# Attention's weighted sums turned by DMA transposes of two 16-bit planes, taken apart and rejoined by GpSimd, instead of by TensorE

## The reference

```python
x = L0_attn_x                                   # (8, 1024, 256)
xn = _layernorm(x)
x = x + _L0_attn_ref(xn, W_kqv) + _L0_ffn_ref(xn, ...)

# attention, per batch b and head h
score = jnp.einsum('bhsd,bhnd->bhsn', q, k) / 16 + slope[h] * (n - s)
attn = jax.nn.softmax(score, axis=-1)
out = jnp.einsum('bhsn,bhnd->bhsd', attn, v)
```

## Time and profile before

| | |
|---|---|
| median of three runs | 2458.93 us |
| span of the profiled execution | 2465.2 us |
| TensorE busy | 2399.8 us, 97% |
| VectorE busy | 1899.4 us, 77% |
| ScalarE busy | 1561.3 us, 63% |
| GpSimd busy | 782.9 us, 32% |
| mean DMA rate | 93 GB/s |

### The profile page before, as it was taken

The page is one execution under the profiler, slowest core; times in us unless marked ns, Lnnn a source line. Parts: engine busy times, 40 slices in busy tenths (PEclk is TensorE's granted clock), DMA queues, the critical chain, the costliest instruction groups (busy, mean ns, idle before and its releaser), DMA issues.

```text
span 2465.2 us, 53774 instructions
## 1 busy us (share of the span) xinstructions
PE 2399.8 (97%) x19426; PEld 1490.7 (60%) x19426; DVE 1899.4 (77%) x2889; ACT 1561.3 (63%) x3276; POOL 782.9 (32%) x901
## 2 busy tenths in 40 slices
PE   8999999996999999989999999999999999999998
PEld 7888888886999999963333333333333333333333
DVE  6666566655556555568999999999999999999994
ACT  3333333333343333315888888888888888888888
POOL 2222323225242222210113333333333333333333
PEclk9999999997999999987999999999999999999999
DMA  6999877771332222232425343434344443435321
GB/s 189 185 166 176 172 129 148 140 120 35 87 98 76 76 75 76 77 74 47 84 49 103 62 88 71 87 72 84 74 79 80 74 85 72 87 67 91 64 58 40
DMA packets 177924, 229.05 MB, mean 93 GB/s; under 512 B 42828, under 2 KB 127436, under 8 KB 177656
## 3 DMA queue, kind: packets, MB, share of 16 engines
q1 hardware_dynamic: 153048, 172.02, 37.6%
q0 software_dynamic: 22448, 50.56, 8.6%
q10 hardware_dynamic: 2176, 3.02, 0.3%
HBM read 131.47 MB, written 93.66 MB: 91 GB/s over the span
## 4 chain that ended last, share of the span: by engine, by line
PE 52%; DVE 2%; DMA 1%; ACT 0%; issue 0%; SPq 0%; DVEq 0%; ACTq 0%
PE p_o L1430 23%; PE p L1418 18%; PE p L1405 9%; PE p L1442 1%; DVE part L1255 1%; DMA q_op<-m_row 1%; PE p L1411 1%; ACT probs L1379 0%; SPq L1144 0%; ACT o_sb L1367 0%; DVE neg L1263 0%; DVE att L1282 0%; DVE att L1302 0%; ACT o_t L1357 0%; DVE rec L1279 0%
## 5 line engine op out<-in xcount | busy, mean ns | idle before, releaser
L1255 DVE TENSOR_REDUCE part<-p 128x2 f32<-128x1024 f32 x1024 | 1237.8, 1221 | 79.9 <-PE p L1405 64.8
L1379 ACT ACTIVATE probs<-p 128x512 f32<-128x512 f32 x2048 | 1109.2, 596 | 159.6 <-PE p L1418 122.8
L1405 PE MATMUL p<-k_op,q_op 50*128 50x512 f32 x2048 | 757.2, 461 | 14.0 <-DVE part L1255 10.9
L1418 PE MATMUL p<-q_op,k_op 51*128 51x512 f32 x2048 | 756.5, 451 | 1.9 <-DMA q_op<-m_row 0.7
L1430 PE MATMUL p_o<-probs,v_op 128*32 128x256 f32 x8192 | 657.4, 392 | 5.1 <-ACT o_sb L1367 1.3
L1418 PEld LDWEIGHTS p<-q_op,k_op 51*128 51x128 f32 x2048 | 312.6, 186 | 417.3 <-ACT probs L1379 355.9
L1430 PEld LDWEIGHTS p_o<-probs,v_op 128*32 128x32 f32 x8192 | 163.3, 108 | 359.7 <-ACT probs L1379 285.0
L1405 PEld LDWEIGHTS p<-k_op,q_op 50*128 50x128 f32 x2048 | 307.0, 189 | 29.3 <-DVE part L1255 26.1
L1206 POOL TENSOR_TENSOR att<-o_t,rec 128x256 f32<-128x256 f32 x63 | 39.0, 618 | 809.1 <-DVE rec L1271 809.1
L828 POOL DMA_INDIRECT xe<-xn_scratch,ids x135 | 146.3, 1083 | 340.4 <-DMA ids<-lists_scratch 309.9
L921 ACT ACTIVATE gated_e<-p_gate 128x352 f32<-128x352 f32 x135 | 62.8, 465 | 194.9 <-PE p_gate L859 115.6
(11 more groups left out here) (186 smaller groups left out, 4052.7 us busy)
## 6 DMA issues: line engine op xcount, KB each, us to landing
k_op<-qk_scratch SPq DMA_DIRECT2D x192, 128.0 KB
q_op<-qk_scratch SPq DMA_DIRECT2D x192, 128.0 KB
yr_scratch<-x SPq DMA_DIRECT2D x135, 128.0 KB
qk_scratch<-k_op SPq DMA_DIRECT2D x32, 512.0 KB
qk_scratch<-q_op SPq DMA_DIRECT2D x32, 512.0 KB
v_scratch<-v_op SPq DMA_DIRECT2D x16, 1024.0 KB
v_op<-v_scratch SPq DMA_DIRECT2D x32, 512.0 KB
x<-in_x SPq DMA_DIRECT2D x16, 512.0 KB
```

Of the source, the lines that this page charges most:

```text
L1255: v.tensor_reduce(part[c_ % 2][:, kh, :, qb], p1[use % 2][:], AX.X, ALU.max, negate=True).then_inc(s["s1_read"], 1)
L1379: a.activation(probs[kb % 4][:, h], p2[use % 3][:], ACT.Exp).then_inc(s["s2_read"], 1)
L1405: return t.matmul(p1[use % 2][:, x], q_op[u][lo:lo + S1_ROWS, pair, q0:q0 + P], k_op[u][lo:lo + S1_ROWS, pair, kh * 512:(kh + 1) * 512], s ...
L1418: t.matmul(p2[use % 3][:], k_op[u][lo:lo + S2_ROWS, pair, kb * P:(kb + 1) * P], q_op[u][lo:lo + S2_ROWS, pair, half * HQ:(half + 1) * HQ], ...
```

## The change

The turn leaves TensorE and ScalarE. GpSimd's `split` copies the two 16-bit halves of each 32-bit value of `o_sb` into two planes `o_pl` (two copies of 128 x 512 values of 16 bits). SP's `turn_output` turns both planes with one DMA transpose (128 x 1024 values of 16 bits, 256 KB) into `o_x`. GpSimd's `rejoin` puts the halves together again in `o_t` (two copies of 128 x 272). VectorE's `invert` of a turn moves later, to the max unit at w = 1 or 17 of one half further on, and so does GpSimd's `normalise`, now one turn behind `split`. The arithmetic is the same.

```diff
-        OUT_COPY, OUT_TURN, OUT_SEEN = (1, 3), 13, 11
+        OUT_COPY, OUT_SEEN = (1, 3), 1
...
+            def turn_output(x_no):
+
+                sp.wait_ge(s["o_pl_ok"], x_no + 1)
+                if x_no >= 2:
+                    sp.wait_ge(s["o_out"], x_no - 1)
+                sp.dma_start_transpose(o_x[x_no % 2][:].rearrange("p t q r -> p (t q) r"),
+                                       o_pl[x_no % 2][:].rearrange("p t q -> p (t q)")
+                                       ).then_inc(s[f"o_x_in{x_no % 2}"], 16)
...
                 send_max(g, u, 1, use2(g, OWN_TURN) + 1)
+                if has_prev:
+                    turn_output(2 * g - 1)
                 if has_next:
                     send_max(g + 1, following(u, turn)[0], 0, use2(g, TURN_AT) + 1)
+                turn_output(2 * g)
...
+            def split(x_no):
+
+                u = x_no % 2
+                pool.wait_ge(s["o_ok"], 2 * x_no + 4)
+                if x_no >= 2:
+                    pool.wait_ge(s[f"o_x_in{u}"], 16 * (x_no // 2))
+                src = o_sb[u][:].bitcast(U16).rearrange("p (q t) -> p t q", t=2)
+                g_.tensor_copy(o_pl[u][:, 0], src[:, 0])
+                g_.tensor_copy(o_pl[u][:, 1], src[:, 1]).then_inc(s["o_pl_ok"], 1)
+
+            def rejoin(x_no):
+
+                u = x_no % 2
+                pool.wait_ge(s[f"o_x_in{u}"], 16 * (x_no // 2 + 1))
+                if x_no >= 2:
+                    pool.wait_ge(s["att_ok"], x_no - 1)
+                dst = o_t[u][:].rearrange("p q h c -> p (q h c)").bitcast(U16).rearrange(
+                    "p (q h c t) -> p t q h c", q=4, h=GH, t=2)
+                src = o_x[u][:].rearrange("p t q (h c) -> p t q h c", h=GH)
+                g_.tensor_copy(dst[:, 0], src[:, 0, :, :, 0:HD + 1])
+                g_.tensor_copy(dst[:, 1], src[:, 1, :, :, 0:HD + 1]).then_inc(s["o_out"], 1)
...
             for x_no in range(2 * GROUPS - 1):
-                normalise(x_no)
+                split(x_no)
+                if x_no:
+                    normalise(x_no - 1)
                 if x_no < NK:
                     last_batch(x_no)
                 if x_no >= NK - 1:
-                    pool.wait_ge(s["att_ok"], x_no + 1)
+                    pool.wait_ge(s["att_ok"], x_no)
                     combine(x_no - (NK - 1))
                 if NK - 2 <= x_no < first + NK - 2:
                     fetch(x_no - (NK - 2))
+                rejoin(x_no)
+            normalise(2 * GROUPS - 2)
...
-                        if w == half * (MAX_UNITS // 2) + OUT_SEEN and (half or has_prev):
-                            invert(2 * g + half - 1)
+                        if w == half * (MAX_UNITS // 2) + OUT_SEEN and has_prev:
+                            invert(2 * g + half - 2)
...
-                    elif n % HALF == OUT_TURN and (half or has_prev):
-                        turned_copy(*((g, 0) if half else (g - 1, 1)), use + 1)
...
-                    if l == OUT_TURN and (half or has_prev):
-                        turn_output(*((g, 0) if half else (g - 1, 1)), use + 1)
```

More of the change, by code:

```diff
@@ L19 @@
 I32 = mybir.dt.int32
+U16 = mybir.dt.uint16
 ALU = mybir.AluOpType
@@ L1069, in attend @@
         o_sb = [sb(f"o_sb{i}", [P, HQ]) for i in range(2)]
+        o_pl = [sb(f"o_pl{i}", [P, 2, HQ], U16) for i in range(2)]
+        o_x = [sb(f"o_x{i}", [P, 2, 4, P], U16) for i in range(2)]
         o_t = [sb(f"o_t{i}", [P, 4, GH, HD + 1]) for i in range(2)]
@@ L1083, in attend @@
                  "pool_c o_st0 o_st1 att_ok o_out base_in0 base_in1 yg_in0 yg_in1 fin_base fin_y "
-                 "dve_f fin_ok fin_st")
+                 "dve_f fin_ok fin_st o_pl_ok o_x_in0 o_x_in1")
         s = {n: sem("t_" + n) for n in names.split()}
@@ L1104, in turns_at @@
         def turns_at(g):
-            out = [OWN_TURN] + [h * HALF + OUT_TURN for h in range(2) if g or h]
-            return sorted(out + ([TURN_AT] if g < GROUPS - 1 else []))
+            return [OWN_TURN] + ([TURN_AT] if g < GROUPS - 1 else [])
         def use2(g, n):
@@ L1325, in group @@
                     last_terms()
+                    invert(2 * g)
                     dve.wait_ge(s["att_ok"], 2 * GROUPS - 1)
@@ L1348, in row_copy @@
                 a.copy(m_row[half][:], p2[use % 3][0:8 * PAIRS, 0:P]).then_inc(s["s2_read"], 1)
[L1350 to L1359, removed]
             def output_copy(g, half, side):
@@ L1365, in output_copy @@
                     act.wait_ge(s["pv_side"], g * 2 + half + 1)
+                x_no = 2 * g + half
+                if x_no >= 2 and side == 0:
+                    act.wait_ge(s["o_pl_ok"], x_no - 1)
                 cols = slice(side * SIDE, (side + 1) * SIDE)
```

## The result

The changed kernel is slower: 2530.15 us median against 2460.05, ratio 1.0286, 95% interval 1.0261 to 1.0312. The forecast was 2440, faster. On a second chip the same kernel took 2508.65 and 2519.23 us in its fast runs, against 2446.34 before the change; two slow runs of 2550.28 and 2582.74 us are not compared.

What follows compares the result with a forecast made beforehand. TensorE's instruction stream was taken to set the pace; -36.5 (turns removed) + 12 (rows delayed) + 4 (odd transpose) = -20.5 us, profiled 2465.2 to about 2445, so median 2438.4, rounded to 2440, range 2424 to 2452.

Steps and rivals of the forecast that it cites:

- The stream: TensorE's instruction stream: 63 turns leave it at 0.58 us each, 36.5 us off.
- GpSimd's traffic in the burst: GpSimd's store moves into the operand-load burst, delaying the rows for unit 32: 0.4 us per group, 12 us.
- The odd transpose: Half 1's turn of the group before, due at VectorE's inversion at w = 17: 4 us charged in all.
- x + R: Odd turn's transpose transfer (x, 2.2 us) plus GpSimd's rejoin (R, 1.2): 3.4 us, free up to 3.9 per group.
- The rival of 8192 pieces: Odd transpose moves as 32-byte destination pieces, x = 10.2 us: 217 us lost, 2652 us; chance 0.15.
- its data run after the burst: SP's queue: odd transpose, issued at about 1517.5 behind loads and rows, starts its data at the burst's end, U - 1.0.
- The first rival: Unit 32: GpSimd's moved traffic and longer list delay the rows 1.5 us, not 0.8; 2459 us; chance 0.13.
- the late transpose: VectorE's inversion at w = 17 waits, TensorE stops once per group; 2516 us at x = 5.5; chance 0.25.
- PE waiting for `q_op<-m_row` in most groups for 0.4 us: Sign that the forecast is right: TensorE waits this long for the row DMAs.
- VectorE's wait ahead of the inversion at w = 17: Sign of being wrong: VectorE waits for GpSimd's rejoin there in every group, not at w = 1.

Runs made afterwards that it cites:

- e7: The change with the rows of half 1 and the odd transpose issued ahead of the operand loads; 2414.86 us, 0.9874 of the kernel before.
- e6: The kernel before with only the rows of half 1 moved ahead of the operand loads; 2445.83 us, 0.9997 of the kernel before.
- e3: The change with its DMA transpose replaced by a copy of 4 bytes per partition; 2427.66 us, 0.9917 of the kernel before.
- e1: The change with the odd transpose issued only after the rows landed, VectorE's inversion four max units later; 2423.73 us, 0.9889 of the kernel before.
- e2: The change with its DMA transpose replaced by a plain copy of the same 256 KB; 2425.99 us, 0.9902 of the kernel before.
- e4: The change with GpSimd's combine, store and fetch behind its rejoin, out of the load burst; 2420.07 us, 0.9882 of the kernel before.
- e12: e4 with SP's loads held until unit 4 is read, so the burst ends later; 2428.02 us, 0.9936 of the kernel before.
- e9: The kernel before with the rows of half 1 held back until unit 31 is read; 2706.65 us, 1.1064 of the kernel before.
- e5: The change with only the rows of half 1 moved ahead of the operand loads; 2629.27 us, 1.0779 of the kernel before.
- e8: e1 with GpSimd also waiting for the rows before it combines in odd turns; 2425.18 us (one run), kernel before 2444.86.
- e14: e1 with GpSimd's odd-turn store held until the rows landed and the odd transpose until unit 34 is read; 2437.16 us (one run), kernel before 2468.85.

## Why the prediction was wrong

The sum was -36.5 + 12 + 4. Its terms:

- **The stream, -36.5 us: right in the stage.** e7 shows it free of everything else: against e6 on the same chip 1203.31 - 1168.90 = 34.4 us over 29 groups, 58 turns, 0.59 each. The whole kernel gained 30.0 us (2444.86 - 2414.86); what the missing us are was not followed.
- **GpSimd's traffic in the burst, 12 us: about right.** e3 has it alone: its waits for the rows grow from 3.9 to 20.6 us on PEld and from 0.7 to 8.8 on PE, and it gains 21.5 us on the kernel before, 8.5 less than e7's 30.0. The sum without the transpose's 4 us says 24.5.
- **The odd transpose, x + R = 3.4 and 4 us charged: its own time was right enough, and the 4 us it was charged are nowhere to be seen.** The pieces are 1024 packets, here of 256 B; a lone transpose takes 1.4 us where I had 2.2; the rejoin takes 1.0 where I had 1.2 and the split 1.2 where I had 2.3; VectorE was not made to wait in the change. The rival of 8192 pieces is dead. The Trainium skill's 1309 ns for a 128 x 128 block (VectorE: DVE Perf Modes, The three transpose paths) can't be taken eight times: eight blocks in one DMA take 1.4 us of transfer here and 3.1 with the latency. The Trainium skill's other figure, 350 to 400 GB/s (Advanced Engine Details and Errata, X-Bar Transpose (TRN2)), is above the 210 GB/s of e1.
- **The step that failed** is in the sentences "SP issues the transpose behind loads and rows" and "its data run after the burst". I asked what the transpose waits for and took for granted that what stands in front of it in the queue is not touched by it; its effect on the rows stands in the sum at nothing. The runs show the opposite. Its data do not run after the burst: its packets begin 17.8 us after the group's start (median), and the rows land at 21.75. With loads and rows unfinished in front and GpSimd's packets beside it, TensorE stood up to 2.9 us for the rows (e1, e2, e3, e4 and e12 each take one part away, and the long waits go).
- **The second step that failed** is the price of a wait. All rivals priced a stop of TensorE at its own length. In the change 45 us of new idle time, 29 of them at unit 32, came with 62 us more of busy time at the lower clock (1228.11 against 1165.95 in e7): 107 us, which makes -36 into +71. e9 shows the clock's share without any DMA transpose.
- The first rival, "The burst eats it", had the right place, the rows at unit 32, but blamed GpSimd's traffic alone and came to 2459. The measured 2530 lies within the 2465 to 2590 given to the late transpose; that is chance, since what that rival says did not happen in the change.
- Of the signs listed, "PE waiting for `q_op<-m_row` in most groups for 0.4 us" is about what e3 has; the change has it 18 times with up to 3.4 us. "VectorE's wait ahead of the inversion at w = 17" came in e5 and, with 5.7 us in all, in e8.

What stays open is why the engines stand still. That a transpose goes in step over all 16 DMA engines, each held until the last has come to it, fits e4's thin stretch and its absence in e14. e1 has one more sign for it. One of its even transposes, from 1756 to 1760 us, has nothing of the program beside it, only one packet of an instruction queue:

```profile
GB/s 0 0 0 0 0 49 172 218 223 200 223 210 189 387 205 179 166 138 33 0 0 0 3 8 5 10 10 10 10 8 13 119 0 0 0 0 0 0 0 0
...
q8 instruction: 1, 0.02, 1.4%
```

For 1.2 us the traffic falls to 13 GB/s and less, and the transpose takes 2.6 us in place of 1.4. By the packet records 12 of e1's 63 transposes overlap such a packet of 8 or 16 KB, and single 256 B packets in them take up to 1455 ns; in the 51 others none takes over 145. So one foreign packet seems to be able to hold a transpose, though no run took it away. But no run here shows the engines one by one, and why GpSimd's packets lengthen the hold behind the loads was not tried further.

## What to carry to other kernels

A DMA that nobody is waiting for can still delay the one in front of it: before placing a DMA transpose, ask what is unfinished ahead of it in its queue and what the other queue moves at that time, and issue it into an empty queue (e7) or after the urgent transfer has landed (e1). A transfer with less than 1 us of slack on the path of TensorE is a risk worth more than its length, since a stop of about 3 us was followed by 17 us at about half the clock, and one of 1.5 us (e12) by a half group at 0.74 of it. So move the urgent small transfers and the transposes ahead of the bulk loads that have 20 us to spare, both of them: moving the rows alone made it worse.

## What the runs showed of the hardware that was not expected

- A transpose of 256 KB from SBUF to SBUF alone (e1): 1024 packets of 256 B, 1.4 us, about 210 GB/s, landing 3.1 us after issue; with one packet of 8 or 16 KB of an instruction queue beside it, up to 2.75 us. With loads unfinished in front of it, DMA traffic fell to 8 to 45 GB/s for 1 us (e4), and with GpSimd's packets too to 75 GB/s and less for some 3.6 us (the change), with the engines counted as busy.
- TensorE's granted clock: in the group of the change shown above, TensorE stood for 2.91 us, and then the granted clock was 0.50 to 0.55, the lower level of 1.2 GHz, from 2099 to 2116 us. Shorter stops are not safe, nor do they always cost: of the change's 18 stops at unit 32 the ten of 1.65 us and more were each followed by a stretch at the lower level, of 3.4 to 20.5 us, and the eight of 1.38 us and less by none; but one of 1.50 us in e12 was, and one of 1.62 in e3 and one of 1.85 in e2 were not.
- GpSimd reads 512 16-bit values per partition that lie 4 bytes apart in 617 ns (1.2 ns each, the split), and writes 272 of them 4 bytes apart in 499 ns (1.8 ns each, the rejoin).
